# Two conditioned linear-attention layers on one core: the turns of y and of q gathered into one group each

## The reference

```
def layer(x, cond):
    xn = layernorm(x) * scale + bias
    q, k, v = xn @ Wq + bq, xn @ Wk + bk, xn @ Wv + bv   # masked rows: k very negative, v zero
    q = softmax(q, over the columns of a head)
    k = softmax(k, over the rows)
    att = k.T @ v                                        # per head
    y = q @ att                                          # per head
    scale, shift = split(silu(cond) @ W_film + b_film)
    h = silu(layernorm(y) * (1 + scale) + shift)
    return x + h @ W_out + b_out
```

## Time and profile before

| | |
|---|---|
| median of 3 runs | 920.95 us (920.02 to 922.26) |
| the profiled execution, its own time | 920.86 us |
| its span in the profile | 918.7 us |
| PE busy in the span | 895.4 us |
| DVE, ACT, POOL busy | 598.9, 398.6, 283.4 us |

### The profile page before, as it was taken

One profiled execution on the slowest core, in us unless ns is written; L12 is line 12 of the kernel. 1 busy time (PEld: TensorE's weight loads), 2 busy tenths in 40 slices (PEclk: granted clock), 3 DMA queues, 4 the chain that ended last, 5 costly groups with the idle time before them and its releaser, 6 DMA issues.

```text
span 918.7 us, 16124 instructions
## 1 busy us (share of the span) xinstructions
PE 895.4 (97%) x5994; PEld 747.5 (81%) x5994; DVE 598.9 (65%) x1293; ACT 398.6 (43%) x607; POOL 283.4 (31%) x305
## 2 busy tenths in 40 slices
PE   4989999999999999999999999999999999999998
PEld 3768888888888888887788888888888888888876
DVE  5757756675676667656696666656756576576764
ACT  5326345434443534344363544335335343444433
POOL 2013423314242231424124342142422314242520
PEclk9989999999999999999999999999999999999999
DMA  6643030020302003032540401203020030301202
GB/s 213 231 181 139 2 137 0 40 97 0 137 0 103 34 0 137 0 138 56 190 187 1 149 1 47 91 0 137 0 107 30 0 137 0 137 0 49 89 1 91
DMA packets 20813, 70.94 MB, mean 77 GB/s; under 512 B 4857, under 2 KB 4905, under 8 KB 14641
## 3 DMA queue, kind: packets, MB, share of 16 engines
q1 hardware_dynamic: 20784, 70.56, 20.1%
HBM read 53.78 MB, written 16.78 MB: 77 GB/s over the span
## 4 chain that ended last, share of the span: by engine, by line
PE 95%; DVE 2%; issue 1%; ACT 0%; POOL 0%; SPq 0%; DVEq 0%; ACTq 0%
PE psum_w L395 57%; PE psum_k L395 19%; PE psum_k L620 6%; PE psum_t L610 3%; PE psum_t L445 3%; PE psum_t L458 3%; PE psum_k L585 3%; PE psum_t L422 1%; PE psum_t L431 1%; DVE x_in L686 0%; DVE y L971 0%; DVE k_max L875 0%; DVE gate L756 0%; DVE w_low_q L694 0%; DVE y_stats L978 0%
## 5 line engine op out<-in xcount | busy, mean ns | idle before, releaser
L1146 POOL TENSOR_TENSOR xT_low<-xT,xT_high 128x512 fp32r<-128x512 f32 x60 | 77.2, 1286 | 214.0 <-ACT xT_high L1040 212.5
L908 DVE TENSOR_TENSOR q<-psum_w,bias_q 128x512 f32<-128x512 f32 x64 | 44.2, 691 | 98.4 <-PE psum_w L395 98.4
L395 PE MATMUL psum_k<-w_high_k,xT_high 128*128 128x512 f32 x256 | 104.7, 409 | 0.5 <-DVE y L971 0.5
L395 PE MATMUL psum_w<-w_high_v,xT_high 128*128 128x512 f32 x256 | 101.3, 396 | 0.2 <-DVE emb_cols L881 0.2
L1063 ACT ACTIVATE gate<-psum_t,film_shift,film_scale 128x512 f32<-128x512 f32 x60 | 46.6, 776 | 126.5 <-PE psum_t L458 95.9
L395 PE MATMUL psum_k<-w_high_k,xT_low 128*128 128x512 f32 x256 | 100.3, 392 | 0.0
L395 PE MATMUL psum_w<-w_high_q,xT_high 128*128 128x512 f32 x256 | 100.1, 391 | 0.0
L395 PE MATMUL psum_k<-w_low_k,xT_high 128*128 128x512 f32 x256 | 100.0, 391 | 0.0
L395 PE MATMUL psum_w<-w_low_v,xT_high 128*128 128x512 f32 x256 | 99.7, 389 | 0.0
L395 PE MATMUL psum_w<-w_high_v,xT_low 128*128 128x512 f32 x256 | 99.7, 389 | 0.0
L395 PE MATMUL psum_w<-w_high_q,xT_low 128*128 128x512 f32 x256 | 99.6, 389 | 0.0
(11 more groups left out here) (129 smaller groups left out, 1835.5 us busy)
## 6 DMA issues: line engine op xcount, KB each, us to landing
x_in<-x_between_layers SPq DMA_DIRECT2D x9, 1024.0 KB, 4.8
x_res<-in_x SPq DMA_DIRECT2D x8, 1024.0 KB, 6.7
x_between_layers<-x_res SPq DMA_DIRECT2D x8, 1024.0 KB, 3.8
x_in<-in_x SPq DMA_DIRECT2D x7, 1024.0 KB, 4.8
x_res<-x_between_layers SPq DMA_DIRECT2D x7, 1024.0 KB, 6.8
out_x<-x_res SPq DMA_DIRECT2D x7, 1024.0 KB, 3.8
raw_weights<-in_L_cond_film_emb_W SPq DMA_DIRECT2D x4, 1024.0 KB, 5.9
raw_weights<-in_L_cond_W_emb SPq DMA_DIRECT2D x4, 1024.0 KB, 5.2
```

Of the source, the lines that this page charges most:

```text
L395: mm = pe.matmul(bank, lhs[:, c, rows_of_tile], rhs[w][:, c, :], start=(c == 0 and n == 0), stop=(c == CHUNKS - 1 and n == 2))
L908: dve.tensor_tensor(q[:, t, :], psum_w[:, t % 2, :], bias_q[:, :], ALU.add)\
L1146: pool.tensor_tensor(xT_low[:, c, :], xT[:, c % 2, :], xT_high[:, c, :], ALU.subtract)\
```

## The change

All four chunks of y are turned in one group, between K tile 2 and K tile 3: chunks 0 and 1 into the banks of `psum_w`, chunks 2 and 3 into those of `psum_t`. V tiles 0 and 1, which write `psum_w`, now wait until `activate` has read the bank. All four tiles of q are turned in one group after output projection 2 and ahead of `attend(0)`: tiles 0 and 1 into `psum_t`, tiles 2 and 3 into banks 2 and 3 of `psum_k`. `attend(1)`, which writes those banks, waits until all four copies to `qT` are done. On DVE, `add_residual` of tile 0 moves ahead of the building of `att`.

```diff
+        def y_bank(c):
+            return (psum_w[:, c, :] if c < 2 else psum_t[:, c - 2, :, :].rearrange("p t s -> p (t s)"))
+        def q_bank(t):
+            return psum_t[:, t, :, :].rearrange("p c s -> p (c s)") if t < 2 else psum_k[:, t, :]
...
             def turn_y(j, c):
...
-                if c < 2:
-                    pe.wait_ge(xT_ready, CHUNKS * (min(j + 2, ITERS) if isinstance(j, int) else j + 2) - 1 + c)
-                else:
-                    pe.wait_ge(gate_ready, CHUNKS * j + c - 1)
-                for t in range(TILES):
-                    mm = pe.transpose(psum_t[:, c % 2, t, :], y[:, t, c * P:(c + 1) * P], ident[:, :])
+                if c == 0:
+                    pe.wait_ge(q_biased, TILES * (j + 1))
+                    if not fixed(j, 0):
+                        pe.wait_ge(o_added, TILES * j)
+                elif c >= 2:
+                    pe.wait_ge(xT_ready, CHUNKS * (j + 2) + c - 3)
+                for t in range(TILES):
+                    mm = pe.transpose(y_bank(c)[:, t * P:(t + 1) * P], y[:, t, c * P:(c + 1) * P], ident[:, :])
...
                         if with_output and t == 3:
-                            turn_y(i - 1, 0)
-                            turn_y(i - 1, 1)
+                            for c in range(CHUNKS):
+                                turn_y(i - 1, c)
...
                 def v_projection(t):
+                    if t < 2 and with_output:
+                        pe.wait_ge(gate_ready, CHUNKS * (i - 1) + t + 1)
...
-                if with_output:
-                    turn_y(i - 1, 2)
-                    turn_y(i - 1, 3)
                 v_projection(0)
...
-                    else:
-                        pe.wait_ge(qT_ready, TILES * i + t - 1)
                     for c in range(CHUNKS):
-                        mm = pe.transpose(psum_t[:, t % 2, c, :], q[:, t, c * P:(c + 1) * P], ident[:, :])
+                        mm = pe.transpose(q_bank(t)[:, c * P:(c + 1) * P], q[:, t, c * P:(c + 1) * P], ident[:, :])
...
                 def attend(t):
                     pe.wait_ge(qT_ready, TILES * i + t + 1)
                     if t == 0:
                         pe.wait_ge(att_ready, i + 1)
+                    if t == 1:
+                        pe.wait_ge(qT_ready, TILES * (i + 1))
...
-                turn_q(0)
-                turn_q(1)
                 if with_output and with_next:
                     out_projection(out_layer, i - 1, 2)
-                turn_q(2)
-                turn_q(3)
+                for t in range(TILES):
+                    turn_q(t)
...
                 if with_next:
                     next_xn(i + 1)
+                if with_output:
+                    add_residual(i - 1, 0)
                 dve.wait_ge(att_done, i + 1)
...
                     mm.then_inc(att_ready, 1)
-                if with_output:
-                    add_residual(i - 1, 0)
```

More of the change, by code:

```diff
@@ L1062, in activate @@
                 cond = bass.ds(j, 1)
-                act.activation(gate[:, c % 2, :], psum_t[:, c % 2, :, :].rearrange("p t s -> p (t s)"), ACT.Silu,
+                act.activation(gate[:, c % 2, :], y_bank(c), ACT.Silu,
                                scale=film_scale[:, cond, c:c + 1].rearrange("p a c -> p (a c)"),
@@ L1114, in iteration @@
                     act.wait_ge(qT_psum, TILES * i + t + 1)
-                    act.copy(qT[:, t, :, :], psum_t[:, t % 2, :, :]).then_inc(qT_ready, 1)
+                    act.copy(qT[:, t, :, :].rearrange("p c s -> p (c s)"), q_bank(t)).then_inc(qT_ready, 1)
                     if fixed(i, LAST_0) and t == 1:
```

## The result

| | before | after |
|---|---|---|
| median | 920.65 us (920.02 to 922.26, 6 runs) | 926.93 us (926.03 to 929.49, 6 runs) |
| ratio | | 1.0072 [1.0057, 1.0087] |
| the profiled execution, its own time; its span | 920.86; 918.7 us | 926.68; 924.5 us |

The change makes the kernel 0.7% slower, 6.3 us by the medians; the forecast was 926.6 us, 5.7 us more. One execution of the kernel before that was taken with the experiments was slow as a whole, 1134.91 us at a mean granted clock of 0.754, and stands in none of the ratios.

A forecast was written before the change was run, and what follows sets the result against it. PE, busy 895.4 of 918.7 us, was taken to bound the kernel. Terms 1.8 + 2.2 + 0.8 + 0.9 = 5.7 us on 920.9 gave 926.6 us, 8-in-10 range 923.0 to 929.8.

The forecast's parts named there:

- waits of `attend(1)` outweigh what the groups save: Second attend, per iteration: 0.23 us lost waiting for q copies and restarting, against 0.03 and 0.06 us gained by grouping.
- the term of the plain iterations: Iterations 1 to 6 and 8 to 14: net loss of 0.14 us each, 1.8 us in all.
- The gain of the groups: PE gains per iteration 0.03 us from one y group less and 0.06 us from one q group less.
- Iteration 7: `attend(1)` waits for ACT's four weight roundings ahead of tile 3's copy: 2.1 us more, 2.2 us with the usual 0.14.
- Iteration 15, building of `att`: Residual 0 goes first on DVE, so `att` is late and `attend(0)` starts at 889.53, against 888.78: 0.8 us.
- Iteration 15, V tile 2: V tile 2 has no slack there, so K tile 3's 0.87 us delay comes through whole: 0.9 us, bounds 0 and 2.2.
- My other bound: V tile 2 of iteration 15: the later split may wait for one POOL addition more, 1.37 us; upper bound 2.2 us.
- V tile 2 waits in every iteration: Rival: V tile 2's weight load waits, its slack being only 0.09 us; 927.9 to 929.2 us; chance 14%.
- faster through changes of kind: Rival: tiles behind turns run slower throughout, so 29 fewer groups save from 0.24 us each; 917.8 us at 0.35; chance 5%.
- The change does nothing: Rival: copies out of four different banks are faster and `attend(1)` doesn't wait; about 921.5 us; chance 5%.
- Single places cost nothing: Rival: later waits take up the one-off losses of iterations 7 and 15; about 923.5 us; chance 9%.
- The clock falls: Rival: turns and attends run at half clock in 14 iterations, costing 46 us: 973 us; chance 2%.

The follow-up runs named there:

- q half alone: Kernel before with only the four q tiles turned in one group and DVE's new order, y as before; 926.81 us, ratio 1.0064.
- all four repairs: Changed kernel plus: x turns before `attend(1)`, iteration 7's roundings before the copies, iteration 15's `att` before residual 0, gate split before tile 3's greatest k; 919.05 us.
- `att` first at 15: Changed kernel, with `att` built ahead of residual 0 in iteration 15 alone; 926.65 us, ratio 1.0062.
- x before `attend(1)`: Changed kernel, with the first eight turns of x between `attend(0)` and `attend(1)`; 922.10 us, ratio 1.0014.
- three repairs: Changed kernel plus: x turns before `attend(1)`, iteration 7's roundings before all q copies, iteration 15's `att` before residual 0; 919.43 us, ratio 0.9984.
- roundings first: Changed kernel, with ACT's weight roundings of iteration 7 ahead of all four q copies; 924.92 us, ratio 1.0041.
- y alone: Kernel before with only the four y chunks turned in one group, q and DVE's order as before; 920.94 us, ratio 1.0004.
- gate split first: Changed kernel, with DVE's split of gate chunk 0 ahead of the greatest k of tile 3; 928.08 us, ratio 1.0079.

## Why the prediction was right

**That waits of `attend(1)` outweigh what the groups save**: right. The q half alone gives 1.0064, and with the turns of x as cover the plain iterations fall from +0.20 to -0.05 us.

**Its sizes**: the term of the plain iterations was 0.14, measured 0.20. The wait with its restart is 0.25 to 0.27 us and not 0.23; 0.02 of it is that the two copies out of `psum_k` take 1.09 and not 1.07 us. The gain of the groups is smaller than 0.03 + 0.06, and is shared out otherwise. From the first turn of y to V tile 1 it takes 7.20 us on average in the changed kernel and 7.25 before, a gain of 0.05 for 0.03, because K tile 3 takes 2.81 us and not 2.85; but V tile 3 comes later by 0.01 to 0.05 us, 0.02 on average, so a part is given back. The q group gains 0.03 for 0.06: output projection 2 takes 2.73 us and not 2.71, and before the change this stretch took 4.50 us and not 4.51. With the gate split ahead of the greatest k, V tile 3 keeps it, and the kernel with all four repairs gains 0.09 us in the average iteration, which is the sum of the two terms. So the sum was right as what PE can save, the two terms were not, and a part of the first was lost to the later gate.

**Iteration 7**: right, 2.4 for 2.2, and the repair takes back 2.1. The four roundings took 2.19 us and the wait 2.09.

**Iteration 15, building of `att`**: the first attend was put at 889.53, that is 3.07 us behind the first turn of q, and came 2.90 behind it, since `att` is built in 1.95 us there (892.41 to 894.36) and not in 2.13. With the 0.07 of the restart the term measures 0.58 + 0.07 = 0.7 for 0.8.

**Iteration 15, V tile 2**: mis-sized, 0.9 forecast, 0.2 measured, and none of that by the later tile. The step that failed is "the 0.87 us of the later K tile come through whole". They don't. DVE's split of gate chunk 0 ends with the POOL addition beside which it starts, and that is the same addition whether K tile 3 comes 0.87 us later or not. Iteration 15 of all ten kernels, in us from its first K matmul (POOL: start of the first of its four additions; the addition: the one that runs beside the split; V tile 2: its first matmul):

| kernel | POOL starts | split starts | addition ends | split ends | V tile 2 |
|---|---|---|---|---|---|
| before | 10.46 | 13.02 | 14.24 (third) | 14.79 | 18.66 |
| after | 10.65 | 13.85 | 14.45 (third) | 15.00 | 18.87 |
| `att` first at 15 | 10.37 | 13.89 | 14.17 (third) | 14.71 | 18.59 |
| x before `attend(1)` | 10.22 | 13.84 | 14.01 (third) | 14.56 | 18.44 |
| three repairs | 10.26 | 13.85 | 14.04 (third) | 14.59 | 18.47 |
| roundings first | 10.27 | 13.89 | 14.06 (third) | 14.61 | 18.48 |
| y alone | 10.21 | 13.89 | 14.01 (third) | 14.57 | 18.46 |
| q alone | 10.76 | 12.99 | 13.29 (second) | 13.84 | 18.45 |
| gate split first | 10.46 | 10.65 | 11.75 (first) | 12.30 | 18.47 |
| all four repairs | 10.64 | 10.60 | none | 11.29 | 18.42 |

In the nine kernels in which an addition runs when the split starts, the split ends 0.54 to 0.56 us behind the end of that addition; alone it takes 0.68 us. Where the third addition is the one, V tile 2 starts 3.87 to 3.89 us behind the split's end. A split that starts 0.83 us later only waits that much less. What sets V tile 2 then is when POOL starts. That hangs on when `x_res` has landed (the release in the rows below), which differs by 0.4 us between kernels that do the same there; why, stays open. The 0.2 us between before and after are POOL's 10.65 for 10.46, and not the cost of the later tile.

It is only just so. In the kernel before the split started 0.03 us behind the end of the second addition, 12.99, when the third already ran. In *q alone*, which has K tile 3 as early as the kernel before and POOL 0.30 us later, the split started beside the second addition, and V tile 2 did not wait: it came 0.42 us sooner than in the changed kernel. So the later tile can cost some 0.4 us here when POOL starts a few tenths later, and costs nothing in this pair of traces. My other bound, one addition more at 5.47 / 4 = 1.37 us, took the mean for the length: the additions start 1.25 us apart and take 1.29 us, only one that starts while a split still runs takes longer, 1.74 to 1.79.

The timeline of the changed kernel:

```profile
861.95 5.50 POOL L1184 TENSOR_TENSOR x_res<-x_res,bias_o 128x512 f32<-128x512 f32 x4 [6.03 <-DMA x_res<-x_between_layers]
...
864.46 1.29 POOL L1184 TENSOR_TENSOR x_res<-x_res,bias_o 128x512 f32<-128x512 f32 x1
...
865.15 1.15 DVE L835 TENSOR_TENSOR gT_low<-gate,gT_high 128x512 fp32r<-128x512 f32 x1
...
865.71 1.74 POOL L1184 TENSOR_TENSOR x_res<-x_res,bias_o 128x512 f32<-128x512 f32 x1
```

The first row holds all four additions, the two of x1 are its third and fourth, from narrower windows of the timeline. In iteration 7 of the same kernel, where nothing of POOL's runs beside it, the split is:

```profile
414.49 0.68 DVE L835 TENSOR_TENSOR gT_low<-gate,gT_high 128x512 fp32r<-128x512 f32 x1
```

The timeline of the kernel with three repairs:

```profile
857.19 5.48 POOL L1187 TENSOR_TENSOR x_res<-x_res,bias_o 128x512 f32<-128x512 f32 x4 [5.63 <-DMA x_res<-x_between_layers]
...
860.78 0.74 DVE L836 TENSOR_TENSOR gT_low<-gate,gT_high 128x512 fp32r<-128x512 f32 x1
```

The timeline of the kernel with all four repairs, where the split starts first, takes no longer than alone, and makes the addition wait instead:

```profile
856.02 0.69 DVE L836 TENSOR_TENSOR gT_low<-gate,gT_high 128x512 fp32r<-128x512 f32 x1 [1.15 <-ACT gT_high L1076]
856.05 1.81 POOL L1187 TENSOR_TENSOR x_res<-x_res,bias_o 128x512 f32<-128x512 f32 x1 [6.01 <-DMA x_res<-x_between_layers]
```

The Trainium skill, "SBUF — State Buffer", section "SBUF: two separate sides", says that a VectorE operation with two SBUF inputs and a GpSimd operation that reads SBUF lock each other out for the whole instruction, and that the one that starts first goes first. The ten rows agree, with 0.55 us of the split's 0.68 left behind the addition's end. Had I followed that to its end (the later split still ends with the same addition), the term would have been 0, the lower bound that I gave.

**The rivals.** *V tile 2 waits in every iteration* and *faster through changes of kind* are refuted by the gate experiment and by the kernels without waits: 0.09 us an iteration with its two groups less, not the 0.24 us a group that it took. *The change does nothing* is refuted by the timeline of iteration 6: the two copies out of `psum_k` take 1.09 us, no less than the 1.07 of before, and the second attend's weight load waits for them. *Single places cost nothing* is refuted by the repairs of iterations 7 and 15. *The clock falls* had one grain of truth, behind iteration 7 in some runs. That the 5.7 us came out so close is luck, because two errors cancel: 0.8 too little in the plain iterations, 0.8 too much in iteration 15.

## What to carry to other kernels

A group that saves changes of kind can take away the cover under which another engine drained the banks, as it did here: sum the drain (here four copies at 0.48 us) against what PE has left to do until the first user of the last bank, and move independent PE work, here the eight turns of x, into that gap before grouping. Look for one-off work in the streams of the engines that PE then waits for (the roundings ahead of ACT's third copy in iteration 7 and residual 0 ahead of DVE's `att` in iteration 15 cost 2.1 and 1.15 us, together as much as 13 waits of 0.25), because its cover may be gone too. The saving itself is small, 0.09 us of 54 per iteration, so a single uncovered wait of 0.25 turns the sign.

## What the runs showed of the hardware beyond this

**A half-clock stretch behind the pause in some runs.** In the experiment with `att` first in iteration 15, PE paused for 2.09 us in iteration 7 behind turns and attends, and then fell to the 1.2 GHz level. Its timeline:

```profile
458.49 1.47 PE L628 MATMUL psum_k<-att,qT 128*128 128x132 f32 x8 [2.09 <-ACT qT L1123]
459.75 1.91 PE L452 MATMUL psum_t<-ident,x_in 128*128 128x128 f32 x8
```

Its window there (the granted clock stands behind POOL's column):

```profile
458.95:462.35 3.40, 3.40 (x17) 3.20 (x17) 2.99 (x6) 1.47 (x3) 0.00 (x0) 0.53 0.70 245
```

The same window view of the changed kernel's profiled execution:

```profile
457.50:461.00 3.50, 3.45 (x23) 3.20 (x24) 3.42 (x7) 1.81 (x3) 0.33 (x1) 1.00 0.60 218
```

Both had the same 2.09 us pause; one fell and one did not, and iteration 7 cost 4.0 us in the one, 2.4 in the other. Of the 22 runs of the four kernels with this pause, 11 show a mean granted clock of 0.994 and 11 one of 0.995 to 0.998. Of the 49 runs of the five kernels without it (no pause there, or the one of 1.22 us) none is below 0.995. Runs of one kernel at 0.994 took 1.4 to 2.7 us longer by their medians than its others (927.87 against 925.20 us with `att` first, 928.10 against 925.48 with the gate split first). These means are of whole runs. A run with a short half-clock stretch in iteration 0 (below) and a fall in iteration 7 would show 0.996, like one with a long stretch and no fall. So 11 is the least number of falls, the 49 runs show no fall only by their means, and where a run fell is seen in the profiled executions alone. In all ten profiled executions, that of the kernel before among them, a PE pause of 3.31 or 3.32 us in iteration 0 is followed by a half-clock stretch as well. That the pause brings it on is supported by these counts; I tried no pause of another length at the place of iteration 7 but the one of 1.22 us, so which of the pause and the turns and attends around it decides, and why only half of the runs fall, stays open. The prediction had this as its last rival, for the groups themselves; in no profiled execution did they bring it on without the pause.

**The half-clock stretch of iteration 0 differs between executions.** In iteration 0 the half-clock stretch was 6.8 us long before and 3.4 us in the changed kernel's profiled execution:

```profile
63.90:67.30 3.40, 3.40 (x18) 3.40 (x18) 2.42 (x7) 1.17 (x2) 0.00 (x0) 0.50 0.49 185
```

Iteration 0 is 0.6 us shorter there than before. In the other eight traces, all with a stretch of 6.8 us, it lies between 0.27 us shorter and 0.24 longer, so most of the 0.6 us is likely the clock's; it is as much as a term of the sum. With the landing of the parameters (up to 1.2 us later than in the trace of before) this is why terms below 1 us were read here from iteration to iteration, and not from the ends of two spans.
